# One order for five engines: new due times and durations in the planner of a recurrence, attention and mixture-of-experts kernel

## The reference

```
x = x + LN(recurrence(LN(x)))
x = x + LN(transformer(LN(x)))

recurrence:  p = x W_state^T + b_state;  g = sigmoid(x W_gate^T + b_gate)
             state = tanh(p_t + state) over 1024 steps, out_t = g_t * state
transformer: h = rms(x) n1;  q, k, v in 16 heads of 16, q and k through rms
             causal softmax(q k^T / 4) v, times wo^T, first 64 columns set to 0, added to x
             xf = rms(x) n2;  gates = top 2 of softmax(xf gate_w^T) over 4 experts
             o0 = gelu(xf e0_up^T) e0_down^T
             o1 = (silu(xf e1_w1^T) * (xf e1_w2^T)) e1_down^T
             o2 = gelu(gelu(gelu(xf l1^T) l2^T) l3^T) l4^T
             o3 = gelu(gelu(xf e3_down^T) e3_up^T) e3_out^T
             x + weighted sum of the four (first 64 columns of it 0)
```

## Time and profile before

| what | value |
|---|---|
| three runs | 1590.9, 1593.12, 1577.78 us; median 1590.9 |
| the profiled execution | 1589.69 us, its span 1588.0 us |
| mean granted clock of TensorE | 0.933 of full |
| TensorE (PE) | 1403.0 us busy, 88% of the span |
| VectorE (DVE) | 1098.6 us, 69% |
| ScalarE (ACT) | 952.3 us, 60% |
| GpSimd (POOL) | 319.2 us, 20% |
| DMA engines, mean | 56.6% |
| chain that ended last | PE 34%, DVE 5%, ACT 4%; its costliest line is L1042, the matmuls |

### The profile page before, as it was taken

The page is one execution under the profiler, slowest core; times in us unless marked ns, Lnnn a source line. Parts: engine busy times, 40 slices in busy tenths (PEclk is TensorE's granted clock), DMA queues, the critical chain, the costliest instruction groups (busy, mean ns, idle before and its releaser), DMA issues. The chain is left out here.

```text
span 1588.0 us, 33694 instructions
## 1 busy us (share of the span) xinstructions
PE 1403.0 (88%) x12320; PEld 1108.8 (70%) x12320; DVE 1098.6 (69%) x2916; ACT 952.3 (60%) x2092; POOL 319.2 (20%) x1146
## 2 busy tenths in 40 slices
PE   6915679999979799998998999999999999999997
PEld 3404567889867568688885577876686667857697
DVE  7776577553886975858888569786788777773342
ACT  2535465675556777775555673538546676468941
POOL 3343333223333323232332110001000010000000
PEclk9956578999998999899998899999999999999999
DMA  5585336754675545546656455665656657556343
GB/s 170 147 285 151 112 103 195 217 152 142 181 227 184 184 138 169 184 125 201 204 177 191 150 161 168 223 193 153 205 178 207 202 170 216 180 189 202 123 144 112
DMA packets 244276, 278.54 MB, mean 175 GB/s; under 512 B 37136, under 2 KB 167696, under 8 KB 243856
## 3 DMA queue, kind: packets, MB, share of 16 engines
q1 hardware_dynamic: 244112, 276.39, 56.6%
HBM read 234.18 MB, written 43.45 MB: 175 GB/s over the span
## 5 line engine op out<-in xcount | busy, mean ns | idle before, releaser
L1702 POOL TENSOR_TENSOR AD<-PX 128x8 f32<-128x8 f32 x1023 | 250.4, 245 | 553.3 <-ACT PX L928 537.3
L928 ACT ACTIVATE PX<-AD 128x8 f32<-128x8 f32 x1023 | 219.3, 214 | 232.0 <-POOL AD L1702 229.8
L996 ACT ACTIVATE work<-PS 128x1024 f32<-128x1024 f32 (+1 forms) x312 | 288.7, 960 | 79.5 <-PE PS L1042 77.8
L1501 DVE TENSOR_REDUCE mx<-PS 128x2 f32<-128x1024 f32 (+3 forms) x256 | 256.7, 1020 | 81.0 <-PE PS L1042 79.9
L1042 PE MATMUL PS<-work,vlx 128*32 128x256 f32 (+2 forms) x2816 | 240.6, 381 | 18.3 <-ACT work L996 7.5
L1042 PE MATMUL PS<-EP,u_e_l 128*128 128x256 f32 x1024 | 199.4, 289 | 6.9 <-DVE EP L1367 4.5
L1709 POOL TENSOR_SCALAR_AFFINE_SELECT work<-work 128x512 f32<-128x512 f32 x96 | 63.8, 674 | 638.1 <-ACT work L996 637.9
L1042 PE MATMUL PS<-WB,work 128*128 128x192 f32 x1024 | 181.2, 330 | 3.6 <-ACT work L1021 1.3
L1021 ACT ACTIVATE work<-PS 128x512 f32<-128x512 f32 x176 | 104.2, 596 | 132.7 <-PE PS L1042 131.2
L1042 PE MATMUL PS<-EP,WB 128*128 128x256 f32 x640 | 182.3, 285 | 0.0
L1042 PE MATMUL PS<-KT,QT 64*128 64x512 f32 (+3 forms) x768 | 151.9, 434 | 27.8 <-DVE mx L1501 12.9
(11 more groups left out here) (170 smaller groups left out, 2345.8 us busy)
## 6 DMA issues: line engine op xcount, KB each, us to landing
KT<-ktd SPq DMA_DIRECT2D x112, 512.0 KB, 4.8
WB<-wlo_e_l SPq DMA_DIRECT2D x160, 256.0 KB, 3.0
WB<-wlo_e_up SPq DMA_DIRECT2D x64, 256.0 KB, 3.0
ktd<-KTs SPq DMA_DIRECT2D x128, 128.0 KB, 2.2
WB<-wlo_e_w SPq DMA_DIRECT2D x64, 256.0 KB, 2.9
WB<-wdn_e_down SPq DMA_DIRECT2D x64, 192.0 KB, 2.7
KT<-ktd SPq DMA_DIRECT2D x48, 256.0 KB, 3.5
KT<-ktd SPq DMA_DIRECT2D x32, 384.0 KB, 4.1
```

Source lines behind the costliest of these rows:

```text
L928: eng.activation(cur, AD[n % 2], ACT.Tanh).then_inc(of(*key), 1)
L996: eng.activation(pt[:, :, :, q0:L], two("sc", *a).rearrange("p a (l q) -> p a l q", l=2)[:, :, :, q0:L], ACT.Exp).then_inc(of(*key), 1)
L1501: eng.tensor_reduce(o, two("mxm", *a)[:, :, 0:w], AX, ALU.max, negate=True).then_inc(of(*key), 1)
L1702: eng.tensor_tensor(AD[n % 2], PX[c % 2][:, :, :, t], PX[(n - 1) // L % 2][:, :, :, (n - 1) % L], ALU.add).then_inc(of(*key), 1)
```

## The change

It changes only the inputs of the planner: `HOP`, `DRAIN`, `LOW`, `HIGH`, `STALL` and `STAY`; all of `START` and `AT`; a new table `STREAM` by which TensorE's time counts towards the clock; and durations and latencies of SyncE's transfers and of `sadd`. The operations, what they follow and how many buffers there are stay. Shortened to its core:

```diff
-HOP = 0.06
-DRAIN = 0.25
+HOP = 0.04
+DRAIN = 0.18
...
-WINDOW, LOW, HIGH, FRESH = 3.413, 0.38, 0.75, 80.0
-
-STALL = {"wsh": 0.3, "wsp": 0.45, "gll": 0.45, "kh": 0.12, "pgate": 0.15, "qq": 0.06, "hsc": 0.05, "fin": 0.05, "pln": 0.03, "pu": 0.03}
-STAY = {"pe": 18.5, "act": 7.0}
-
-START = (114.6, 163.8, 192.7, 269.5, 332.7, 421.8, 507.9, 597.9, 743.8, 801.4, 926.0, 996.4, 1096.7, 1187.3, 1295.6, 1383.6)
-AT = {"piece": (-65.1, 79.3, 93.0, 117.5),
-      "post": (73.5, 53.5, -11.6, 4.0),
...
-      "key": (-92.9, -70.4, 23.2, -60.9),
-      "query": (-70.1, -15.7, -105.7, -9.8),
-      "max": (-55.3, -48.9, -46.0, -51.3),
-      "maxima": (1.8, 4.8, 14.5, 33.1),
...
-      "score": (20.8, 39.5, 20.4, 48.1),
...
-      "l1": (38.7, 246.6, 204.8, 191.9),
-      "e0up": (141.5, 167.2, 99.3, 296.6),
-      "l2": (241.4, 262.9, 274.5, 274.1),
-      "e0dn": (304.8, 265.3, 456.7, -58.1),
-      "e1": (248.8, 254.1, 341.0, 226.9),
...
-      "e3up": (250.0, 261.2, 290.1, 275.3),
+WINDOW, LOW, HIGH, FRESH = 3.413, 0.36, 0.78, 80.0
+
+STREAM = {"ptr": 0.6, "qtr": 0.6, "xtr": 0.6, "aot": 0.6, "mgt": 0.6, "mtr": 0.6, "kt": 0.65, "qt": 0.65, "gm": 0.05, "htr": 0.5}
+
+STALL = {"wsh": 0.3, "wsp": 0.5, "gll": 0.45, "kh": 0.12, "pgate": 0.17, "qq": 0.1, "qred": 0.1, "qh": 0.13, "hsc": 0.1, "fin": 0.06,
+         "pln": 0.06, "pu": 0.05}
+STAY = {"pe": 22.8, "act": 1.5}
+
+START = (115.0, 167.5, 171.2, 248.8, 350.1, 440.7, 512.5, 587.1, 735.8, 799.1, 934.5, 1003.1, 1116.8, 1193.1, 1290.9, 1363.9)
+AT = {"piece": (-147.0, 133.0, 82.8, 250.5),
+      "post": (134.5, 36.8, 86.3, 58.5),
...
+      "key": (-126.2, -70.5, 53.2, -61.6),
+      "query": (-83.7, -4.6, -147.4, -50.6),
+      "max": (-115.2, -53.4, -43.3, -43.8),
+      "maxima": (-84.8, 10.4, 12.5, 38.9),
...
+      "score": (-11.4, 34.1, 27.9, 46.8),
...
+      "l1": (-62.8, 317.2, 241.6, 193.2),
+      "e0up": (98.6, 175.1, 102.1, 390.0),
+      "l2": (251.4, 257.0, 244.9, 519.2),
+      "e0dn": (335.6, 257.3, 474.8, -10.4),
+      "e1": (272.9, 241.9, 342.4, 254.9),
...
+      "e3up": (272.0, 376.2, 341.6, 458.1),
...
-                        streamed[w] += t - t0
+                        streamed[w] += (t - t0) * STREAM.get(k[0], 0.95)
...
-            add("pool", ("sadd", n), 0.20, -1000.0, ("stanh", n - 1), *px)
+            add("pool", ("sadd", n), 0.235, -1000.0, ("stanh", n - 1), *px)
...
-            add("sp", ("kst", u, s), 1.0, d, ("kc", u, s), lat=2.5)
+            add("sp", ("kst", u, s), 2.45, d, ("kc", u, s), lat=2.2)
...
-            add("sp", ("wr", u, name, h, k), 0.35, d, *([("wr", *prior["wr"])] if "wr" in prior else [("wst", w) for w in PIECES]),
-                *([] if name in UPS else [("wdd", name)]), lat=4.0, take={"W": (until,)})
+            add("sp", ("wr", u, name, h, k), 0.39, d, *([("wr", *prior["wr"])] if "wr" in prior else [("wst", w) for w in PIECES]),
+                *([] if name in UPS else [("wdd", name)]), lat=2.7, take={"W": (until,)})
```

More of the change, by code:

```diff
@@ new lines @@
+AT = {"piece": (-147.0, 133.0, 82.8, 250.5),
+      "post": (134.5, 36.8, 86.3, 58.5),
+      "prep": (17.1, -19.8, -78.7, 116.5),
+      "value": (-221.7, 57.6, -159.3, -133.7),
+      "key": (-126.2, -70.5, 53.2, -61.6),
+      "query": (-83.7, -4.6, -147.4, -50.6),
+      "max": (-115.2, -53.4, -43.3, -43.8),
+      "maxima": (-84.8, 10.4, 12.5, 38.9),
+      "bound": (-44.5, -55.4, 66.6, 100.8),
+      "score": (-11.4, 34.1, 27.9, 46.8),
+      "scores": (15.9, 13.0, 19.1, 8.0),
+      "av": (22.7, -42.6, 7.9, 7.5),
+      "merge": (34.8, -43.0, -32.5, -18.4),
+      "out": (-165.5, 12.8, -239.6, -89.0),
+      "gate": (-166.4, -52.5, 16.6, -20.2),
+      "l1": (-62.8, 317.2, 241.6, 193.2),
[3 more added lines that the diff above has]
+      "e1": (272.9, 241.9, 342.4, 254.9),
+      "l3": (274.9, 254.3, 181.8, 267.8),
+      "e3dn": (221.9, 342.7, 211.7, 282.7),
+      "e1dn": (278.1, 353.1, 278.8, 331.6),
+      "l4": (266.5, 300.1, 185.9, 310.5),
+      "e3up": (272.0, 376.2, 341.6, 458.1),
+      "e3out": (230.9, 261.3, 192.6, 417.8),
+      "fin": (192.1, 92.1, 143.4, 473.4)}
@@ L298, in arrange @@
             if staged:
-                add("sp", ("hsv", n, gate), 0.35, d + 9, (f"hout{gate}", n), lat=3.0)
+                add("sp", ("hsv", n, gate), 0.35, d + 9, (f"hout{gate}", n), lat=3.4)
     add("pool", ("ident",), 1.4, 0.0)
@@ L313, in arrange @@
         add("sp", ("pxl", c), 0.4, 0.0, *[("hsv", 2 * c + s, 0) for s in range(2)], ("stanh", L * (c - 1)),
-            *[("pgate", 4 * (c - 2) + b) for b in range(B)], lat=8.0)
+            *[("pgate", 4 * (c - 2) + b) for b in range(B)], lat=5.6)
     prior = {}
@@ L323, in arrange @@
         last = ("stanh", 128 * rows[1][1] + 127)
[L325 to L326 removed]
+        add("sp", ("gl", u), 0.57 if c else 1.1, d - 20, ("hsv", rows[0][1], 1), ("hsv", rows[1][1], 1), ("wsp", "v"), lat=3.5, take={"G": (("ptr", u),)})
+        add("sp", ("xl", u), 0.4, d - 20, ("ptr", u), lat=3.8, take={"XR": (("x1st", u), ("pu", u))})
         add("dve", ("pgate", u), dve(512), d, ("gl", u), last)
@@ L366, in arrange @@
             dj = d + at["maxima"] * j / len(jobs)
-            add("sp", ("ktm", u, j), 0.35, dj - 5, *keys, *([("ktm", *prior["ktm"])] if "ktm" in prior else []), lat=4.5, take={"KT": (("mxm", u, ends[j]),)})
+            add("sp", ("ktm", u, j), 0.55 if c else 1.1, dj - 5, *keys, *([("ktm", *prior["ktm"])] if "ktm" in prior else []), lat=1.4 + 0.36 * len(planes) * nkb, take={"KT": (("mxm", u, ends[j]),)})
             prior["ktm"] = (u, j)
@@ L389, in arrange @@
             dg = d + at["scores"] * g
-            add("sp", ("vl", u, g), 0.35, dg - 5, *[("vst", w) for w in keys_before(u)], *([("vl", *prior["vl"])] if "vl" in prior else []), lat=4.5, take={"VL": (("av", u, g, nkb - 1),)})
+            add("sp", ("vl", u, g), 0.43 if c else 0.86, dg - 5, *[("vst", w) for w in keys_before(u)], *([("vl", *prior["vl"])] if "vl" in prior else []), lat=1.6 + 0.2 * nkb, take={"VL": (("av", u, g, nkb - 1),)})
             prior["vl"] = (u, g)
@@ L393, in arrange @@
                 lastkb = min(4 * h + 3, nkb - 1)
-                add("sp", ("kts", u, g, h), 0.35, dg - 5, *keys, *([("kts", *prior["kts"])] if "kts" in prior else []), lat=4.5, take={"KT": (("sc", u, g, lastkb),)})
+                add("sp", ("kts", u, g, h), 0.55 if c else 1.1, dg - 5, *keys, *([("kts", *prior["kts"])] if "kts" in prior else []), lat=1.4 + 0.72 * min(4, nkb - 4 * h), take={"KT": (("sc", u, g, lastkb),)})
                 prior["kts"] = (u, g, h)
```

36 lines of the change are left out of this document (10 added, 26 removed).

## The result

The changed kernel takes 1604.3 us (median of 20 runs, 1593.8 to 1610.4) against 1585.3 for the kernel before (20 runs, 1577.8 to 1594.7). The ratio is 1.0113, 95% interval 1.0094 to 1.0133: **slower by 1.1%**, where 1573 and faster was forecast. Of the kernel's own planner: it plays 1598.9 us for the old order and 1574.0 for the new one. The old order came 14 us under its plan, the new one 30 over. That swing of 44 us, against a planned gain of 25, is the thing to explain.

What follows compares the result with a forecast made beforehand. The prediction took the kernel as bound by TensorE's work plus 259 us of holes, only the holes being open to reordering. Terms -15 - 4 + 2 = -17 from 1589.7 gave 1573 us, range 1548 to 1604.

Steps and rivals of the forecast that it cites:

- main term: 300 to 920 us: new clock weights and due times close three of eleven half-clock spots, 5.0 us each, -15 us.
- Transfers, -4: Waits for keys and the maxima row, 16.8 us, shrink by a quarter through truer transfer numbers; bounds 0 to -12.
- bound of +5: Worse case for transfers: loads stand behind stores in the queue that are now issued at a different point, +5 us.
- the prediction's own sign: Half-clock time after 300 us about 60 us instead of 82; as long as before or longer means wrong.
- First 102 us, 0: Start and recurrence before unit 0: no change, as the recurrence's due time stays; bounds 3 us either way.
- 102 to 300 us, 0: Chain of one unit at a time, without other work for TensorE: no change; bounds -10 and +10 us.
- ScalarE's tables, +2: Lower penalty for exp-to-gelu changes gives a fifth more table loads, 22, and longer exp waits; bounds 0 and +15.
- 920 us to the end, 0: All but 42 us already full, so no change; bounds -10 and the price of a slower last maximum stage.
- slower rival: Unit 15's maxima, from about 1375 us, lack FFN fill from units 13 and 14: +23 us, 1613; chance 0.16.
- middle class: Whole kernel counted as the same, between 1575 and 1607 us, about 1% from no change; chance 0.38.

Runs made afterwards that it cites:

- experiment 3: Changed kernel and kernel before, each with FFN weight loads cut to 64 of 256 columns (of 192 for second layers): 1597.4 and 1577.6 us.
- the two with the pair: Kernel before with signal numbers 0.04 and 0.18 and newly searched due times, one search scored over six clock-window positions: 1623.7 us, and 1627.7 for the six-position one.
- experiment 2: Changed kernel and kernel before, each with the score-maximum products of units 4 to 11 carried out twice as fill: 1625.1 and 1603.5 us.

## Why the prediction was wrong

Measured less planned, by numbers and due times: old and old -14 and -8, old and new -7; new and new +30, +40 and +38, new and old +5. The new numbers add 16 us where the due times are old (from a mean of -11 to +5) and 43 where they are new (from -7 to +36). By the planner's own measure they are what turned a planned gain of 25 us into a loss of 19. That holds for the set of new numbers as a whole, under due times near the change's; which of them does it is not shown.

**The step that failed** is the main term, -15 for three slow spots closed between 300 and 920 us, together with the premise under it and under the transfers' -4, that the planner's new numbers are the true ones. The terms in turn:

**Transfers, -4.** I wrote that the new numbers are the true ones, from a median issue time and four stores in the earlier trace rows. As medians they are near (an issue of 0.33 us where the plan has 0.39, a landing of 2.90 where it has 3.1). But a product waits for the later of two pieces, and a list in fixed order waits for each load that is late and gets nothing for each that is early; such a price leaves 39% of the weight loads late. It also has no landing between a store and the load that reads it back in the same queue. How much this costs is not shown, and experiment 3 speaks against much for the weight loads. Waits for keys and the maxima row rose from 16.8 to 20.0 us (17.8 and 2.2), where I had 13; all transfer waits from 25 to 42. My bound of +5, "loads behind stores in the queue", named the spot that then showed at 230 us. That the new transfer numbers have a part in the slip between 200 and 345 us is argued from its kind (transfer waits of 12 to 18 us in all of five lists made with them, 0.8 to 1.2 in the three made with the old, 4.1 and 5.9 in the two with the pair); 6.9 us of these waits are planned, and a kernel in which the transfer numbers alone were put back wasn't run. Nor is it one property of the loads: a quarter of the bytes won 2 us, a freer head of the queue nothing.

**300 to 920 us, -15: the main step.** By the prediction's own sign it failed: the half-clock time after 300 us is 116 us, not the 60 of the forecast nor the 82 of before, in seventeen spots and not in eight. The ledger has +11.4 between 300 and 920 us, and half-clock work costs 18 us more over all after 300. I reasoned that stricter clock thresholds let the search see the slow stretches. It did plan around them: but its low stretches stand at other places than the trace's (297 to 307 us planned, 312 to 329 real). An order that is 16 us late by then has other work at hand than planned where the clock falls. That this lateness makes the extra spots is argued, not shown; filling them up (experiment 2) didn't bring the two orders closer.

**First 102 us, 0:** +0.2, right. **102 to 300 us, 0:** +4.5, inside its bounds; but the slip against the plan begins here, and I had treated the stage as closed because its loss hardly moves.

**ScalarE's tables, +2.** The loads fell by 10 instead of rising by 22; that the due times outweigh a `STAY` of 1.5 is the likely reason, not a tested one. The wait for exp went from 15.3 to 16.2, inside the bounds, but the way to it was wrong: that it fits is luck.

**920 us to the end, 0.** +10.8: the loss after 920 us is 52.7, not beside 42, and five half-clock stretches stand between 990 and 1500 us, where before there was none. I took "full already" as safe from harm. The slower rival didn't happen: the loss of 1200 to 1540 is 20.7 and not 30.

The forecast counted as slower only what is over 1607 us, with 0.14; 1604.3 falls into its middle class, with 0.38, of which the forecast gave only 0.02 to a slowing by the mechanism of its slower rival. Against the 1585.3 of the kernel before the slowing is clear of the noise all the same. The argument that a duration in the planner costs nothing on the chip is true, but it left out that the order is only as good as the durations that it was planned with.

**Open:** which of the new numbers does the harm (transfers, the pair 0.04 and 0.18, or stage constants), why old due times suffer 16 us from them and new ones 43, and what beside the recurrence's round makes the searches with the pair miss their plans by 41 and 51 us. No version that beats the kernel before was found.

## What to carry to other kernels

Check every new set of numbers for a planner first with an order nobody optimised, run on the chip: the two random ones came 40 and 38 us over their plans, the searched one 30. Compare each step's real start with its planned one; the first place where they part tells more than the ledger of losses, which spread the same fault over all stages. Mending one late load in a chain won nothing here. Numbers that make up one round belong together: the new signal time with the old addition made each of the recurrence's rounds some 0.035 us too short, and two orders planned so were 10 us late by 200 us. Whether a transfer should be priced by its late cases rather than its median, these runs leave open.

## What the runs showed beside

Shifting the due times by at most 1 us each costs 60 us (before, one draw) and 80 us (after, two draws) on the chip, and nearly as much in the plans: the orders sit on a very narrow optimum, so a small edit of all due times is not a small change. A store that its own queue reads back holds the queue for 2.6 us after its last issue, and a delay of 5.9 us in the middle of the run costs more at the end (8.4) than the same delay early (4.0), though their intervals overlap (1.0 to 6.8 and 5.2 to 11.6).
